# A two-layer macaron block: attention sums kept unturned, reciprocals taken in one small tile, four single banks for the maxima and three for the scores

## The chip, the cores and the metric

The kernel runs on one core of one Trainium2 chip. The metric is the device time of one execution in microseconds (us). Five engines work side by side, each through its own queue in order: TensorE (PE, with its weight loads shown apart as PEld), VectorE (DVE), ScalarE (ACT), GpSimd (POOL) and SyncE (SP), which issues the transfers. They meet at semaphores only. Matmuls write to PSUM, here eight banks of 128 partitions by 512 float32 columns; DVE and ACT read the banks.

## What is computed

The input `x` is 2 x 2048 tokens of 256 features. The reference is a feed-forward, a causal attention and the same feed-forward again, each added to `x`:

```python
x = x + 0.5 * ffn(layernorm(x), W_fc, W_proj)       # relu squared, 1024 hidden, then 5 spiking steps
x = x + attn(layernorm(x), Wq, Wk, Wv, bv, Wo, bo)  # 16 heads of 16, rotary q and k, causal softmax
x = x + 0.5 * ffn(layernorm(x), W_fc, W_proj)
```

The attention is `softmax(q k' / 4, causal) v` for each head, and its output goes through `Wo`. All is float32; products that must be exact are made of three matmuls of high and low parts.

## The kernel before

The program has three stages. The **first feed-forward** takes the tokens in 8 chunks of 512, with projections to q, k and v behind it. The **attention** takes 8 groups (`GROUPS`): 2 sequences by 4 groups of 4 heads. A group has 4 steps `j` of 512 queries, and step `j` has `4j + 4` blocks `b` of 128 keys, so 40 blocks a group (`BLOCKS`) and 320 in all. The **second feed-forward** takes 8 chunks again, with the output projection of the attention ahead of each (`attn_turn`, `attn_out`). All five engines walk the same list of 320 slots, one for each block, each in its own program order.

In slot `g` PE issues (lines 1107 to 1122): some units, the scores of heads 0 and 1, some units, the scores of heads 2 and 3, some units, the products of block `g - 2`, some units. A **unit** (line 1035) is one matmul of queries with keys for one head that only serves to find the largest score of each query; it fills one of `MB = 3` banks of `m_ps`, and DVE takes the maximum out of it (line 971 without mask, line 974 on the diagonal). There are 160 units in a group, placed by `place_units` in the 20 slots before and the 20 after the group's first, mostly 4 or 5 in a slot. The unit `i` may start once DVE has read unit `i - MB`. After the last unit of a step DVE negates the maxima and a **shift** item turns them on PE (line 1052), and SP puts them into the queries as extra rows.

The **scores** (line 1067) of two heads `par = 0, 1` go to the two banks of `s_ps[hp]`, one for each head; the matmuls of `par` 0 and 1 use the upper and the lower half of the array's rows. ACT takes the exponential of both banks in one instruction of up to 1024 columns (line 950). Pair `hp` of block `g` may be written once pair `hp` of block `g - 1` has been read:

```python
wait(pe, exp_done, 2 * block_no(n, j, b) + hp - 1)
```

The last four blocks of a step lie on the diagonal and are 512, 384, 256 and 128 columns wide; POOL sets the masked part to zero. The **products** (line 1082) are the four heads' probabilities times the values, with a column of ones beside the values, so that row 16 of each head's 32 rows in `o_ps` holds the sum of probabilities. At the end of a step ACT copies `o_ps` to `osum` (line 938). A **sums** item then turns `osum` on PE into a bank of `m_ps` (4 transposes, line 1064), DVE takes the reciprocals and multiplies (lines 1005 and 1008), and SP stores token-major `att`. These items stand in the same ring of banks as the units: in slots 7, 15 and 27 of a group and in slot 3 of the next.

In the second feed-forward `load_attn` (line 141) reads the token-major result, PE turns it (8 transposes, line 605), ACT rounds it to `mT_hi` (line 248), DVE makes `mT_lo` (line 362) and `attn_out` projects. Within a chunk's eight steps `f` DVE has its normalisation in `f == 4`, `mT_lo` in `f == 6` and `xT_lo`, for which PE's next chunk waits, in `f == 7` (lines 442 to 489). The first two chunks are prepared within the last group's slots by the `lead` functions.

## Time and profile before

| | |
|---|---|
| median of 3 runs | 1481.79 us (1480.66 to 1482.88) |
| the profiled execution | 1480.84 us |
| its span, first to last instruction | 1479.1 us |
| busy in the span | PE 91%, DVE 77%, ACT 58%, POOL 15% |
| mean granted TensorE clock | 0.949 of 2.4 GHz |
| chain that ended last | PE 74%, DVE 19%, ACT 4% |
| first feed-forward alone | 0 to 309 us |
| its end beside the first units | 309 to 405 us, PEclk 0.67 |
| 300 slots with units | 405 to 1200 us |
| last 20 slots, without units | 1200 to 1252 us |
| second feed-forward | 1252 to 1479 us |

The profiled execution's time lies 1.7 us over its span, and 0.95 us under the median. In the profile a line such as L1049 is the line of the kernel. A busy PE is not a PE at its peak: a matmul's time there includes its weight load and its way through the array, and two matmuls on different halves of the rows overlap.

### The profile page before, as it was taken

What the parts mean: (1) busy time and instruction counts of PE and PEld (TensorE: products, weight loads), DVE (VectorE), ACT (ScalarE), POOL (GpSimd) and SP (SyncE); (2) the same over time, 40 slices, a digit from 0 to 9 for tenths busy, and PEclk for the clock granted to TensorE, in tenths of its full rate; (3) what the DMA queues carried; (4) which work ended last, traced back from release to release, by engine and by line L of the source; (5) the groups of instructions that cost most, each with busy time, mean ns of one, the idle gap of its engine ahead of it and who ended that gap; (6) DMA issues with size and microseconds to landing.
All of it is one profiled execution on the core that took longest, in us unless ns stands there. A gap on an engine that the chain in (4) does not pass through costs nothing.

```text
span 1479.1 us, 22638 instructions
## 1 busy us (share of the span) xinstructions
PE 1345.1 (91%) x8416; PEld 809.8 (55%) x8416; DVE 1134.0 (77%) x2686; ACT 861.4 (58%) x1157; POOL 223.7 (15%) x205
## 2 busy tenths in 40 slices
PE   4988888967799999999999999999999998999996
PEld 3877777854444343444444444443443433999996
DVE  6566776796788888898898898888888851576675
ACT  4654455511166666676666666666666668665664
POOL 4002222241210110110110110110210110101100
PEclk9999999976699999999999999999999999999998
DMA  3123443772272160250340420610701011232312
GB/s 110 48 81 119 136 135 122 149 209 93 72 109 29 27 92 6 39 75 6 56 59 6 75 40 5 91 24 5 106 9 44 9 33 47 76 100 87 99 44 72
DMA packets 98598, 101.41 MB, mean 69 GB/s; under 512 B 39260, under 2 KB 78940, under 8 KB 96860
## 3 DMA queue, kind: packets, MB, share of 16 engines
q1 hardware_dynamic: 98488, 99.97, 29.7%
q8 instruction: 66, 1.08, 0.3%
q14 instruction: 44, 0.36, 0.1%
HBM read 60.16 MB, written 37.75 MB: 66 GB/s over the span
## 4 chain that ended last, share of the span: by engine, by line
PE 74%; DVE 19%; ACT 4%; issue 3%; DMA 0%; POOL 0%; SPq 0%; DVEq 0%; ACTq 0%
PE m_ps L1049 20%; PE o_ps L1094 18%; DVE maxes L971 9%; PE yps_c L563 6%; PE ups_c L545 6%; PE s_ps L1078 5%; PE ups_a L545 5%; PE yps_a L563 4%; PE gps_a L594 3%; DVE masked L974 3%; PE gps_a L579 2%; DVE turned_a L403 2%; PE gps_c L579 2%; ACT probs L950 1%; PE tps_a L572 1%
## 5 line engine op out<-in xcount | busy, mean ns | idle before, releaser
L950 ACT ACTIVATE probs<-s_ps 128x1024 f32<-128x1024 f32 (+3 forms) x640 | 542.0, 896 | 282.6 <-PE s_ps L1078 281.2
L971 DVE TENSOR_REDUCE maxes<-m_ps 128x1 f32<-128x512 f32 x768 | 490.2, 684 | 72.6 <-PE m_ps L1049 70.7
L1049 PE MATMUL m_ps<-kT,qT 64*128 64x512 f32 (+3 forms) x1280 | 455.6, 459 | 56.4 <-DVE maxes L971 37.9
L1049 PEld LDWEIGHTS m_ps<-kT,qT 64*128 64x128 f32 x1280 | 204.2, 192 | 412.1 <-DVE maxes L971 277.6
L1078 PE MATMUL s_ps<-qT,kT 64*128 64x512 f32 (+3 forms) x1280 | 317.0, 404 | 6.8 <-ACT probs L950 6.6
L1094 PE MATMUL o_ps<-probs,v_w 128*32 128x512 f32 (+3 forms) x2560 | 311.1, 559 | 0.1
L974 DVE CUSTOM_DVE_ANT_0 masked<-m_ps,mask 128x384 f32<-128x384 f32 (+3 forms) x512 | 233.6, 485 | 52.7 <-PE m_ps L1049 50.8
L919 POOL TENSOR_SCALAR_AFFINE_SELECT probs<-probs 128x512 f32<-128x512 f32 x128 | 81.3, 635 | 742.0 <-ACT probs L950 742.0
L1078 PEld LDWEIGHTS s_ps<-qT,kT 64*128 64x128 f32 x1280 | 170.0, 192 | 34.0 <-ACT probs L950 28.7
L452 DVE TENSOR_TENSOR h_lo_c<-hsq_c,h_hi_c 128x512 fp32r<-128x512 f32 x64 | 45.0, 703 | 71.1 <-ACT hsq_c L301 35.6
L294 ACT ACTIVATE relu_a<-ups_a 128x512 f32<-128x512 f32 x64 | 38.2, 596 | 99.5 <-PE ups_a L545 98.9
L452 DVE TENSOR_TENSOR h_lo_a<-hsq_a,h_hi_a 128x512 fp32r<-128x512 f32 x64 | 47.3, 739 | 58.5 <-ACT hsq_a L301 36.4
L1094 PEld LDWEIGHTS o_ps<-probs,v_w 128*32 128x32 f32 x2560 | 51.2, 109 | 73.6 <-issue 61.4
L294 ACT ACTIVATE relu_c<-ups_c 128x512 f32<-128x512 f32 x64 | 38.1, 596 | 73.5 <-PE ups_c L545 72.6
L501 POOL TENSOR_TENSOR rot_a<-turned_a 128x512 f32<-128x512 f32 x32 | 42.9, 1362 | 219.9 <-DVE turned_a L403 219.9
L563 PE MATMUL yps_a<-down_hi,h_hi_a 128*128 128x256 f32 x256 | 73.0, 285 | 2.2 <-ACT y_a L288 2.2
L563 PE MATMUL yps_c<-down_hi,h_hi_c 128*128 128x256 f32 x256 | 73.0, 285 | 0.0
L563 PE MATMUL yps_a<-down_lo,h_hi_a 128*128 128x256 f32 x256 | 72.5, 283 | 0.0
L563 PE MATMUL yps_a<-down_hi,h_lo_a 128*128 128x256 f32 x256 | 72.5, 283 | 0.0
L563 PE MATMUL yps_c<-down_hi,h_lo_c 128*128 128x256 f32 x256 | 72.4, 283 | 0.0
L563 PE MATMUL yps_c<-down_lo,h_hi_c 128*128 128x256 f32 x256 | 72.3, 283 | 0.0
L545 PE MATMUL ups_a<-xT_hi_a,up_hi 128*128 128x512 f32 x128 | 54.3, 424 | 2.5 <-DVE xT_lo_a L362 2.5
(128 smaller groups left out, 1923.3 us busy)
## 6 DMA issues: line engine op xcount, KB each, us to landing
qT<-qkT_parts SPq DMA_DIRECT2D x96, 128.0 KB
kT<-qkT_parts SPq DMA_DIRECT2D x48, 256.0 KB
qkT_parts<-qk_hi_a SPq DMA_DIRECT2D x32, 256.0 KB, 4.9
qkT_parts<-qk_lo_a SPq DMA_DIRECT2D x32, 256.0 KB, 4.6
table_a<-in_rot SPq DMA_DIRECT2D x8, 768.0 KB, 7.4
xin_a<-in_x SPq DMA_DIRECT2D x8, 512.0 KB, 3.9
xres_a<-in_x SPq DMA_DIRECT2D x8, 512.0 KB, 4.8
x<-xsum_a SPq DMA_DIRECT2D x8, 512.0 KB, 3.2
```

Of the source, the lines that this page charges most:

```text
L294: act.activation(relu[:, f % 2, :], ups[:, f % 2, :], ACT.Relu).then_inc(s["relu_done"], 1)
L452: dve.tensor_tensor(h_lo[:, f % HB, :], hsq[:, f % 2, :], h_hi[:, f % HB, :].bitcast(F32), ALU.subtract).then_inc(s["lo_done"], 1)
L545: last = pe.matmul(ups[:, f % 2, :], wt[:, c, f * P:(f + 1) * P], x[:, c, :], start=(i == 0), stop=(i == 3 * EC - 1))
L563: last = pe.matmul(yps[:, t, :], h[:, f % HB, t * P:(t + 1) * P], wt[:, f, :], start=(f == 0 and i == 0 and t % 2 == 0), stop=(f == FC - 1 ...
L579: last = pe.matmul(out, x[:, c, t * P:(t + 1) * P], wt[:, c, c0:c1], start=(i == 0), stop=(i == 3 * EC - 1))
L919: pool.affine_select(out=tile, in_=tile, compare_op=ALU.is_ge, fill=0.0, base=0, pattern=[[0, G], [1, P]], channel_multiplier=-1).then_inc ...
L950: act.activation(probs[:, b % PBUF, 2 * hp:2 * hp + 2, off:CH], s_ps[hp][:, :, off:CH], ACT.Exp, scale=D ** -0.5).then_inc(exp_done, 1)
L971: dve.tensor_reduce(out, m_ps[:, i % MB, 0:width], AX.X, ALU.max).then_inc(max_read, 1)
L974: dve.tensor_tensor_reduce(masked[:, i % MB, 0:width], m_ps[:, i % MB, 0:width], mask[:, CH - width:CH], 1.0, NEG, ALU.add, ALU.max, out). ...
L1049: pe.matmul(m_ps[:, i % MB, 0:width], qT[n % 2][r0:r0 + HR, j, hp, t * P:(t + 1) * P], kT[n % 2][r0:r0 + HR, hp, k * CH:k * CH + width], s ...
L1078: mm = pe.matmul(s_ps[hp][:, par, off:CH], kT[n % 2][r0:r0 + HR, hp, b * P:(b + 1) * P], qT[n % 2][r0:r0 + HR, j, hp, off:CH], start=True, ...
L1094: mm = pe.matmul(o_ps[VW * h:VW * (h + 1), off:CH], v_w[n % 2][:, b, h, :], probs[:, b % PBUF, h, off:CH], start=(b == 0), stop=(b == T * ...
```

## The change

The sums are no longer turned. `osum` gets two buffers and is stored as it stands to `sumsT` in DRAM (128 rows a group, transposed). The sums items, `turn_sums` and `normalise` go, and with them the reads of `m_ps` by DVE for them. In the second feed-forward SP loads the sums' rows back into `sums`, already features by tokens, and a copy of the reciprocals of the denominators, spread over 16 rows each, into `denom`. The reciprocals are made once for each chunk on a 128 x 64 tile: SP loads the denominators (`load_denom`), DVE takes the reciprocal (`attn_recip`), SP stores them (`store_recip`). DVE multiplies (`attn_norm`), ACT rounds and DVE makes the low part, both now from SBUF. `attn_turn` goes.

The four banks of scores become three single ones, `s_ps[:, i % 3]`, one for each head in turn. Each head's score matmul signals by itself and waits by itself, and ACT takes one exponential for each head, up to 512 columns. The bank that is freed goes to `m_ps`, which has four.

```diff
-MB = 3
+MB = 4
+SB = 3
...
         def load_attn(c):
...
+            for k in range(EC):
+                sp.dma_start(sums[:, k, :], heads[k, :, 0:D, :]).then_inc(s["a_in"], 16)
+                sp.dma_start(denom[:, k, :], recips[k].unsqueeze(1).broadcast_to([H // EC, D, CH])).then_inc(s["a_in"], 16)
...
+        def attn_recip(c):
+
+            wait(dve, f"denom_in{c % 2}", 16 * (c // 2 + 1))
+            dve.reciprocal(recip[:, c % 2, :], recip[:, c % 2, :]).then_inc(s["a_recip"], 1)
...
+        def attn_norm(c):
+
+            wait(dve, "a_in", 16 * 2 * EC * (c + 1))
+            dve.tensor_tensor(sums[:, :, :], sums[:, :, :], denom[:, :, :], ALU.mult).then_inc(s["a_norm"], 1)
...
                 if f == 4:
                     norm_scale(it + 1)
                     norm("pre", it + 1, it + 1, x2, xn, 0)
+                    if has(it, -2):
+                        attn_norm(it + 2)
+                if f == 5 and has(it, -3):
+                    attn_recip(it + 3)
...
-            if not first and f == 5 and has(it, -2):
-                attn_turn(it + 2)
...
             wait(act, pv_done, g - PBUF + 1)
             for hp in range(2):
-                act.wait_ge(s_done, 2 * g + hp + 1)
-                act.activation(probs[:, b % PBUF, 2 * hp:2 * hp + 2, off:CH], s_ps[hp][:, :, off:CH], ACT.Exp,
-                               scale=D ** -0.5).then_inc(exp_done, 1)
+                for par in range(2):
+                    i = G * g + 2 * hp + par
+                    act.wait_ge(s_done, i + 1)
+                    act.activation(probs[:, b % PBUF, 2 * hp + par, off:CH], s_ps[:, i % SB, off:CH], ACT.Exp,
+                                   scale=D ** -0.5).then_inc(exp_done, 1)
...
-        def turn_sums(e):
-            i = ITEM[e]
-            free_bank(e)
-            pe.wait_ge(o_read, step_no(e[1], e[2]) + 1)
-            for t in range(T):
-                mm = pe.transpose(m_ps[:, bank_of(e), t * P:(t + 1) * P], osum[:, t * P:(t + 1) * P], ident[:, :])
-            mm.then_inc(max_done, 1)
...
-            wait(pe, exp_done, 2 * block_no(n, j, b) + hp - 1)
             for par in range(2):
+                i = G * block_no(n, j, b) + 2 * hp + par
+                wait(pe, exp_done, i - SB + 1)
                 r0 = HR * par
-                mm = pe.matmul(s_ps[hp][:, par, off:CH], kT[n % 2][r0:r0 + HR, hp, b * P:(b + 1) * P],
-                               qT[n % 2][r0:r0 + HR, j, hp, off:CH], start=True, stop=True)
-            mm.then_inc(s_done, 1)
+                pe.matmul(s_ps[:, i % SB, off:CH], kT[n % 2][r0:r0 + HR, hp, b * P:(b + 1) * P],
+                          qT[n % 2][r0:r0 + HR, j, hp, off:CH], start=True, stop=True).then_inc(s_done, 1)
```

The lead of the second feed-forward moves with it: the first two chunks' loads, reciprocals and multiplications stand in slots 2 to 29 of the last group, and the two turns there go.

## Rows read from the trace of the kernel before

**Rows 1.** Windows by stage: length, PE, PEld, DVE, ACT, POOL busy, PEclk, DMA share, GB/s

```profile
405.00:1200.00 795.00, 757.23 (x4921) 323.33 (x4920) 690.52 (x1840) 522.66 (x632) 94.62 (x129) 0.96 0.28 43
1200.00:1252.00 52.00, 46.09 (x311) 17.95 (x312) 10.70 (x27) 39.37 (x48) 9.73 (x10) 0.90 0.18 54
1252.00:1479.00 227.00, 215.55 (x1428) 195.39 (x1426) 147.06 (x260) 133.16 (x222) 17.03 (x6) 0.98 0.25 78
```

**Rows 2.** Waits from 405 to 1200: us in total, times, longest

```profile
DVE maxes L971 <- PE m_ps L1049: 49.5, 142, 0.7
DVE masked L974 <- PE m_ps L1049: 47.9, 97, 1.7
```

**Rows 3.** Timeline of PE's weight loads in one full slot: start us, us, what

```profile
909.94 0.19 PEld L1049 LDWEIGHTS m_ps<-kT,qT 64*128 64x128 f32 x2 [0.84 <-DVE maxes L974]
910.05 0.19 PEld L1078 LDWEIGHTS s_ps<-qT,kT 64*128 64x128 f32 x2
...
911.22 0.18 PEld L1049 LDWEIGHTS m_ps<-kT,qT 64*128 64x128 f32 x1 [0.52 <-DVE maxes L971]
911.65 0.16 PEld L1094 LDWEIGHTS o_ps<-probs,v_w 128*32 128x32 f32 x8 [0.24 <-issue]
912.64 0.19 PEld L1049 LDWEIGHTS m_ps<-kT,qT 64*128 64x128 f32 x2 [0.84 <-DVE maxes L974]
```

**Rows 4.** Timeline of DVE and of ACT in the same slot

```profile
910.48 1.29 DVE L971 TENSOR_REDUCE maxes<-m_ps 128x1 f32<-128x512 f32 x2 [0.20 <-PE m_ps L1049]
...
910.78 1.94 ACT L950 ACTIVATE probs<-s_ps 128x1024 f32<-128x1024 f32 x2 [0.76 <-PE s_ps L1078]
```

**Rows 5.** Groups by shape of line 950: count, busy us, mean ns of one

```profile
L950 ACT ACTIVATE probs<-s_ps 128x512 f32<-128x512 f32 x64 | 35.0, 602 | 14.5 <-PE s_ps L1078 14.5
...
L950 ACT ACTIVATE probs<-s_ps 128x256 f32<-128x256 f32 x64 | 21.2, 381 | 24.1 <-PE s_ps L1078 24.1
```

**Rows 6.** Timeline, last group: exponentials end, two scores that wait, the products behind

```profile
1211.80 3.77 ACT L950 ACTIVATE probs<-s_ps 128x1024 f32<-128x1024 f32 x4 [3.96 <-PE s_ps L1078]
...
1213.79 0.19 PEld L1078 LDWEIGHTS s_ps<-qT,kT 64*128 64x128 f32 x2 [0.73 <-ACT probs L950]
1214.21 0.16 PEld L1094 LDWEIGHTS o_ps<-probs,v_w 128*32 128x32 f32 x8 [0.24 <-issue]
```

**Rows 7.** Timeline, diagonal slot of 256 columns; products of 384 columns and what follows

```profile
932.69 0.29 PEld L1078 LDWEIGHTS s_ps<-qT,kT 64*128 64x128 f32 x2
...
933.36 0.16 PEld L1094 LDWEIGHTS o_ps<-probs,v_w 128*32 128x32 f32 x8
...
934.90 0.16 PEld L1094 LDWEIGHTS o_ps<-probs,v_w 128*32 128x32 f32 x8
935.68 0.19 PEld L1049 LDWEIGHTS m_ps<-kT,qT 64*128 64x128 f32 x2 [0.62 <-DVE maxes L974]
```

**Rows 8.** Timeline of ACT, same diagonal slot

```profile
933.41 1.08 ACT L950 ACTIVATE probs<-s_ps 128x512 f32<-128x512 f32 x2 [1.00 <-PE s_ps L1078]
```

**Rows 9.** First products of two groups in a row, 40 slots apart

```profile
941.00 0.16 PEld L1094 LDWEIGHTS o_ps<-probs,v_w 128*32 128x32 f32 x8 [0.24 <-ACT osum L938]
...
1047.12 0.16 PEld L1094 LDWEIGHTS o_ps<-probs,v_w 128*32 128x32 f32 x8 [0.24 <-ACT osum L938]
```

**Rows 10.** Timeline, the four transposes of a sums item on PE

```profile
943.80 0.42 PEld L1064 LDWEIGHTS m_ps<-ident,osum 128*128 128x128 f32 x4 [0.24 <-issue]
```

**Rows 11.** Waits from 309 to 405

```profile
PE m_ps L1049 <- DVE maxes L971: 21.7, 17, 5.6
```

**Rows 12.** Timeline of DVE, a chunk of the second feed-forward, steps 4 to 7

```profile
1320.70 0.69 DVE L452 TENSOR_TENSOR h_lo_c<-hsq_c,h_hi_c 128x512 fp32r<-128x512 f32 x1 [1.58 <-ACT hsq_c L301]
...
1327.21 0.69 DVE L452 TENSOR_TENSOR h_lo_c<-hsq_c,h_hi_c 128x512 fp32r<-128x512 f32 x1 [0.65 <-ACT hsq_c L301]
...
1330.59 1.22 DVE L362 TENSOR_TENSOR xT_lo_c<-tps_c,xT_hi_c 128x1024 fp32r<-128x1024 f32 x1 [0.42 <-ACT xT_hi_c L248]
```

**Rows 13.** Window at the lower clock, columns as in Rows 1

```profile
1228.00:1232.00 4.00, 4.00 (x20) 0.70 (x12) 1.23 (x1) 3.36 (x5) 0.00 (x0) 0.50 0.37 128
```

More of the change, by code:

```diff
@@ L101, in feed_forward @@
     else:
-        ain, xb, x2, bias = (own[n] for n in ("ain", "xb", "x2", "bias"))
+        sums, recip, denom, xb, x2, bias = (own[n] for n in ("sums", "recip", "denom", "xb", "x2", "bias"))
         split = [("o", own["stage_o"][:, :], proj_hi, proj_lo)]
@@ L222, in body @@
                     store_x2(it + 1)
+                if has(it, -3):
+                    load_denom(it + 3)
+            elif f == FC - 1 and has(it, -3):
+                store_recip(it + 3)
         def end():
@@ L245, in high, with attn_high @@
                 wait(act, "proj_done", 3 * c)
-            if which == "a":
-                wait(act, "o_done", c)
             act.activation(hi[:, :, :], bank[:, :, :], ACT.Copy).then_inc(s[which + "_hi"], 1)
+        def attn_high(c):
+            wait(act, "a_norm", c + 1)
+            wait(act, "o_done", c)
+            act.activation(mT_hi[:, :, :], sums[:, :, :], ACT.Copy).then_inc(s["a_hi"], 1)
         def v_evac(c):
@@ L722, in ring_order @@
             order += [(g, ("unit", n, u)) for u in unit_slots.get(g - BLOCKS * n, [])]
-        order += [(g, ("sums", n, j)) for n in range(GROUPS) for j in range(NJ) if block_no(n, j + 1, SUM) == g
-                  or j == NJ - 1 and block_no(n + 1, 0, SUM) == g]
-    order.append((LAST, ("sums", GROUPS - 1, NJ - 1)))
     for n in range(GROUPS):
@@ L767, in attention @@
     qT, kT, v_in, v_w = ([own[f"{n}{p}"] for p in range(2)] for n in ("qT", "kT", "v_in", "v_w"))
-    probs, ident, bias, mask, masked, maxes, negmax, negparts, shiftT, osum, denom, att = (own[n] for n in (
-        "probs", "ident", "bias_b", "mask", "masked", "maxes", "negmax", "negparts", "shiftT", "osum", "denom", "att"))
+    probs, ident, bias, mask, masked, maxes, negmax, negparts, shiftT, osum = (own[n] for n in (
+        "probs", "ident", "bias_b", "mask", "masked", "maxes", "negmax", "negparts", "shiftT", "osum"))
     s_ps, m_ps, o_ps = banks
@@ L822, in moves @@
                     shift(n, j)
-                elif what == "sums":
+            for n, j in steps():
+                if g == min(block_no(n, j, T * j + T) + STORE, LAST):
                     store(n, j)
@@ L933, in read_sum @@
         def read_sum(n, j):
+            t = step_no(n, j)
             act.wait_ge(pv_done, block_no(n, j, T * j + T))
-            if (n, j) != (0, 0):
-                act.wait_ge(max_done, ITEM["sums", (NJ * n + j - 1) // NJ, (j - 1) % NJ] + 1)
-            act.activation(osum[:, :], o_ps[:, :], ACT.Copy).then_inc(o_read, 1)
+            wait(act, osum_out[j % 2], 16 * (t // 2))
+            act.activation(osum[:, j % 2, :], o_ps[:, :], ACT.Copy).then_inc(o_read, 1)
         def slot(g):
@@ L1126, in end @@
                 products(*SLOTS[g])
-        def last_sums():
-            ring(ITEMS[LAST])
-        return slot, end, last_sums
+        return slot, end
     return sync, scalar, vector, gpsimd, tensor
@@ L1184, in build @@
     b["probs"] = memory.take("probs", [P, PBUF, G, CH])
-    b["osum"] = memory.take("osum", [P, CH])
+    b["osum"] = memory.take("osum", [P, 2, CH])
     assert memory.at <= rest
@@ L1204, in build @@
     memory = Memory(nc, probs)
-    for n in ("xres", "xsum"):
-        c[n] = memory.take(n + "_c", [P, T, E])
+    for n, shape, dt in (("xres", [P, T, E], F32), ("xsum", [P, T, E], F32), ("count", [P, T * E], BF16)):
+        c[n] = memory.take(n + "_c", shape, dt)
     with ExitStack() as ctx:
```

172 lines of the change are left out of this document (84 added, 88 removed).

## The prediction

> **What bounds the kernel now.** I read the windows by stage first, then the waits of the longest stage, then the timelines of one slot, engine by engine. 795 of the 1479 us lie in the 300 slots of attention that have units, 52 in the last 20 slots, 227 in the second feed-forward [rows 1]. In the long stage PE is busy 757 us, DVE 691, ACT 523. So PE and DVE are both near full, and what counts is how they hand over to each other. DVE waited 49.5 + 47.9 = 97 us for units, in 239 waits of 0.4 us [rows 2].
>
> One full slot shows the loop. PE loads two units at 909.94 and the first scores at 910.05, then waits at its last unit until 911.22, because with three banks it must let DVE finish the first unit of this slot; the products start at 911.65 and take 0.99 us, and the next slot's units start at 912.64: 2.70 us [rows 3]. DVE starts on the first unit at 910.48 after 0.20 us of idleness [rows 4]. The loop is: unit to DVE 0.54, DVE's read and the way back 0.74, last unit to products 0.43, products 0.99. ACT is no part of it: it starts the pair's exponential at 910.78, waited 0.76 us for it, and has done by 912.72 [rows 4]. A whole group of 40 slots takes 1047.12 - 941.00 = 106.1 us, 2.65 a slot [rows 9]; the seven such pairs lie between 106.0 and 107.1.
>
> **Four banks for the units and no sums items** take this loop away. The last unit now waits for a unit of the slot before, which DVE has read long ago. A sums item costs PE 0.42 us for its transposes [rows 10], and one unit more waits behind it. If nothing came in its place, the 97 us would shrink and some 0.6 us for each of 30 sums items would go.
>
> **Three single score banks** put a new wait in its place, and this is the step on which I decide. The four scores of slot g have the numbers 4g to 4g + 3, and score i waits until exponential i - 3 is done. So the fourth score waits for the first exponential of its own slot. Before, the second pair waited only for the slot before. The price, from rows:
> - First score's load to ACT's start: 910.05 to 910.78, 0.73 us [rows 3, 4].
> - One exponential of 512 columns: 0.60 [rows 5].
> - End of an exponential to the load of a score that waits for it: the second of four back to back ends at 1211.80 + 0.92 + 1.02 = 1213.74 (four take 3.77, so each but the last adds 0.92), and the load is at 1213.79: 0.05 [rows 6].
> - Load of a late score to the products: 1213.79 to 1214.21, 0.42 [rows 6]. The unit between them shares that time if it uses the other half of the rows.
> - Products 0.99, and products' end to the next first score 0.11 [rows 3].
>
> Together 0.73 + 0.60 + 0.05 + 0.42 + 0.99 + 0.11 = 2.90 us for a full slot, whatever DVE does; it was 2.70. The loop goes PE to ACT to PE once a slot, and PE stands about 1.0 us at the fourth score with the remaining units, the products and all of the next slot queued behind it. DVE has then more than it can use, and ACT, with four exponentials at 0.48 (two take 1.08, one 0.60 [rows 5, 8]) and one tail, needs 2.04 of the 2.90.
>
> On the diagonal the loss is larger, as these slots were short. With 256 columns: first score to ACT 932.69 to 933.41, 0.72 [rows 7, 8]; exponential 0.38 [rows 5]; then 0.05 + 0.42. So the products come 1.57 us after the first score, where they came 0.67 after it [rows 7]. For 384 columns I take 0.62 + 0.49 and for 128 0.60 + 0.27, estimates from the same rows' slope of 0.86 ns a column, with 0.25 instead of 0.42 behind the narrowest.
>
> The group's sum: products 28 x 0.99 + 4 x (0.78 + 0.57 + 0.36) = 34.6 (0.78 for 384 columns, 934.90 to 935.68 [rows 7], 0.21 less for each 128 columns fewer); first score to fourth score 28 x 1.38 + 4 x (1.16 + 1.15 + 0.92) = 51.6; fourth score to products 36 x 0.42 + 4 x 0.25 = 16.1; turn of the slot 40 x 0.11 = 4.4. That is 106.7. On top come units beyond four in a slot, the shift items, and a unit on the same half of the rows as the fourth score: 0 to 5 us, I take 3.7, since ten slots or so have each of these at 0.1 to 0.2. **110.4 for 106.1**, so +4.3 a group. Crowded slots, in which PE waited most for DVE, gain; quiet and diagonal ones lose more. 300 slots are 7.5 groups: **+32 us** (bounds: 0.2 us less or more in the hand-overs of each slot, -28 to +92 against the time before).
>
> **The last 20 slots** have no units. Today ACT binds them with pairs of exponentials at 0.92 each, 1.84 a slot [rows 6]. A full slot now needs 0.60 + 0.60 + 0.05 + 0.42 + 0.99 = 2.66. Fourteen full slots and six diagonal ones come to 50, and the chunk's projection, one turn and ACT's table loads stand in between for some 8: 58 for 52 [rows 1], **+6** (3 to 15).
>
> **The stretch before 405.** PE waited 21.7 us there for DVE to free a bank, in 17 waits [rows 11]. One more bank lets it run one read of 0.6 us further each time, part of which DVE's long work takes back: **-4** (-12 to 0).
>
> **The second feed-forward** is PE's alone. Six turns of 8 transposes (two of the 8 chunks' were in the lead) go, at about 0.42 for four [rows 10]: -5. But DVE gets a multiplication of 128 x 1024 in step 4, for which I take the 1.14 that `xT_lo` adds [rows 12], and a reciprocal of 64 columns in step 5, no row of this size, between 0.2 and 1 us, I take 0.5. From step 4's start at 1320.70 to the end of `xT_lo` at 1331.81 are 11.1 us, and the free time in it is 0.65 + 0.42 [rows 12]; so `xT_lo` comes 0.6 us later, and PE waits for it at the next chunk. The turns' gain is then not to be had: six times 0.5, less 0.6 for the last sums item, **+2** (-6 to +8). The added loads, four for one and two small ones for each chunk, are issued a chunk ahead and hide behind it; SP's queue waits in `load_attn` for a store of reciprocals, with `load_x` and the stores behind, none needed within a step. If that cover failed, a load's few us would stand in front of each of six chunks. Uncovered nowhere: the single `osum` copies and their stores.
>
> **Sum.** 1480.84 + 32 + 6 - 4 + 2 = 1516.8; the median lay 0.95 above the profiled execution: **1518 us**.
>
> A page speaks to the scores' signals: in the Trainium skill, "TensorE: Matmul & The Clock Gate", section "The cost: per-tile semaphore tail", increments of tiles that run side by side serialise at 26 ns each. Each pair now signals twice. An estimate by that page would be 0.03 us in each of 320 slots, 8 us more; no row here parts the two.
>
> **Rival one: the fourth score's wait hides** (0.18). It would if the first exponential's release came 0.2 us earlier than I have it, at 1.18 instead of 1.38 us after the first score: then a full slot is below today's 2.70, and the gain of the banks shows. For it: today's completion is that of a pair, and a single head's may come sooner. Against: both heads stream side by side, and the terms are all measured. With half of DVE's 97 us and half of the sums items' 20 or so gone, the time is about 1420, at the very least 1365.
>
> **Rival two: the clock** (0.13). PE's work in a slot stays, the slot grows, so PE idles more. In the last group the granted clock is 0.50, which is 1.2 GHz, from 1228 to 1232 [rows 13], behind a stretch in which PE had waited for ACT; over the last 20 slots it is 0.90 [rows 1]. At that level products take about 0.9 us longer, and with the scores a slot some 1.3. If 30 to 60 slots fall so, +40 to +75: 1555 to 1590. The Trainium skill says the same, "TensorE: Matmul & The Clock Gate", section "A second HAM failure mode: psum-queue depth-cycling": small idle gaps between groups of matmuls let the clock swing between its levels. By that rule the last 20 slots are the first to fall.
>
> **Rival three: the two loops balance** (0.12): the crowded slots gain what the quiet ones lose. 1479 to 1494; of this 0.05 is within 0.2%, about what a measurement of this kernel can tell from no change.
>
> **How the numbers follow.** Forecast, 1495 to 1545: 0.55. Rival one 0.18, rival two 0.13, rival three 0.12, something slower yet 0.02. Faster 0.18, same 0.05, slower 0.77. The range runs from 1479 to 1572: it holds the forecast, rival three and most of rival two.
>
> **What would show it.** Right: in a full slot of units two loads of scores close together, a third, and the fourth about 1.4 us after the first, with "ACT probs" as its releaser; full slots of 2.9 us and hardly any that differ by their number of units; DVE's waits for `m_ps` not gone but longer, ACT's exponentials in runs of one to three; diagonal slots of 2.3 to 2.8. Wrong: the fourth score's load within 0.5 us of the first, DVE back to back. The second feed-forward is right if PE waits for `xT_lo` by 1 us or more each chunk.

## The result, and the profile after

The changed kernel took **1576.04 us** (1571.72 to 1584.23, 4 runs), the kernel before 1481.32 (1480.66 to 1482.88, 4 runs) beside it: ratio 1.0644, 95% interval 1.0599 to 1.069. Slower, as forecast, but by 95 us where 36 were forecast, and 4 us above the range. The profiled execution took 1577.86 with a span of 1576.1; the four runs order themselves by their mean granted clock: 1571.72 at 0.938, 1574.22 at 0.937, 1577.86 at 0.934, 1584.23 at 0.928.

The windows of the changed kernel, with the columns of [rows 1]:

```profile
405.00:1200.00 795.00, 686.03 (x4424) 280.19 (x4423) 623.80 (x1661) 514.84 (x1127) 86.25 (x116) 0.96 0.28 46
```

In the same 795 us PE gets through 4424 matmuls, before it was 4921. The waits of that window (us in total, times, longest):

```profile
PEld s_ps L1098 <- ACT probs L992: 201.6, 273, 1.2
...
DVE masked L1016 <- PE m_ps L1076: 83.4, 119, 2.5
DVE maxes L1013 <- PE m_ps L1076: 82.0, 139, 1.9
```

Now 273 slots have a score that waits for ACT, 0.74 us each. DVE's waits for units, 97 us in [rows 2], are 165: four m banks did not let DVE run on, since PE, which fills them, stands at the score. One full slot shows it. PE's weight loads:

```profile
1262.01 0.19 PEld L1098 LDWEIGHTS s_ps<-qT,kT 64*128 64x128 f32 x2
...
1262.25 0.18 PEld L1098 LDWEIGHTS s_ps<-qT,kT 64*128 64x128 f32 x1
1263.38 0.18 PEld L1098 LDWEIGHTS s_ps<-qT,kT 64*128 64x128 f32 x1 [0.95 <-ACT probs L992]
...
1263.80 0.16 PEld L1113 LDWEIGHTS o_ps<-probs,v_w 128*32 128x32 f32 x8 [0.24 <-ACT probs L992]
...
1264.91 0.19 PEld L1098 LDWEIGHTS s_ps<-qT,kT 64*128 64x128 f32 x2
```

and ACT's exponentials of the same slot:

```profile
1262.73 2.06 ACT L992 ACTIVATE probs<-s_ps 128x512 f32<-128x512 f32 x4 [0.84 <-PE s_ps L1098]
```

Two scores, a third, and the fourth 1.37 us after the first with ACT's `probs` as releaser; from first score to first score 1264.91 - 1262.01 = **2.90 us**, the forecast's number, against 2.70 in [rows 3]. ACT starts 0.72 after the load. So the mechanism stands, and the question is where the other 60 us are.

These two are slots with nothing on top. Taken over all full slots of this stage that lie at the full clock (512 columns in the scores and in the products; 142 of them after, 140 before), the median goes from 2.71 to 3.06 us and the mean only from 2.97 to 3.09, since the slots before spread from 2.20 to 4.48 and those after from 2.78 to 3.84.

I split both spans at three places: the first products, those 297 slots later, and those of the slot before the last two. Before, the three stand at 409.80, 1197.14 and 1249.79, after at 406.47, 1266.70 and 1335.15. The two middle stretches, before and then after, as windows with the columns of [rows 1]:

```profile
409.80:1197.14 787.34, 752.13 (x4899) 320.85 (x4898) 684.79 (x1825) 517.06 (x625) 93.35 (x127) 0.97 0.28 43
1197.14:1249.79 52.65, 45.48 (x295) 17.30 (x295) 13.24 (x35) 39.48 (x48) 8.71 (x9) 0.90 0.18 54
...
406.47:1266.70 860.23, 742.67 (x4779) 302.67 (x4778) 672.45 (x1769) 555.26 (x1219) 93.23 (x127) 0.95 0.27 44
1266.70:1335.15 68.45, 57.10 (x276) 20.56 (x274) 18.46 (x34) 43.22 (x89) 9.31 (x9) 0.78 0.20 59
```

| stretch | before | forecast | after | after, PE kept at work (experiment e6_fill) |
|---|---|---|---|---|
| to the first products | 409.8 | -4 | -3.3 | -3.8 |
| slots with units | 787.3 | +32 | +72.9 | +46.2 |
| last 20 slots | 52.65 | +6 | +15.8 | +10.9 |
| from there to the end of the span | 229.3 | +2 | +11.6 | +10.0 |
| sum | 1479.1 | +36 | +97.0 | +63.2 |

Between the same products of one group and the next lie 118.7, 114.8, 113.5, 120.4, 112.4, 114.5 and 113.9 us, where before all were within 106.0 to 107.1 [rows 9]. A loop gives every group the same; something in the changed kernel comes and goes. The granted clock goes with it: its mean is 0.90 in the group of 120.4 us and 0.92 in that of 118.7, and 1.00 in that of 112.4. The kernel before is not free of this either: each of its groups has a mean of 0.97 or 0.95. Two windows of 4 us behind the narrow diagonal slots at the start of a group, columns as in [rows 1]:

```profile
520.00:524.00 4.00, 3.32 (x30) 1.68 (x30) 3.76 (x8) 3.42 (x9) 2.10 (x3) 1.00 0.76 169
...
528.00:532.00 4.00, 3.67 (x16) 1.31 (x15) 1.50 (x6) 1.33 (x5) 0.63 (x1) 0.50 0.99 116
```

The granted clock (the column before the last two) falls from 1.00 to 0.50, which is 1.2 GHz, behind slots in which PE waited 0.6 to 0.8 us for ACT each; by 532 it is back. In between full products take 1.86 us:

```profile
525.21 0.20 PEld L1113 LDWEIGHTS o_ps<-probs,v_w 128*32 128x32 f32 x8 [0.24 <-issue]
527.07 0.28 PEld L1076 LDWEIGHTS m_ps<-kT,qT 64*128 64x128 f32 x1 [1.66 <-issue]
```

against 0.99 in [rows 3].

### The profile page after: what moved, and what is told of

Read it like the earlier page. It is cut to its first block and busy times, and to the rows that moved or that the text cites. A ratio compares the mean times of both kernels' runs of the same rounds, so it can differ in the third digit from the quotient of the medians.

```text
span 1576.1 us, 22827 instructions
## 1 busy us (share of the span) xinstructions
PE 1344.9 (85%) x8224; PEld 792.7 (50%) x8224; DVE 1135.1 (72%) x2638; ACT 902.6 (57%) x1797; POOL 222.5 (14%) x205
## 5 line engine op out<-in xcount | busy, mean ns | idle before, releaser
L992 ACT ACTIVATE probs<-s_ps 128x512 f32<-128x512 f32 (+3 forms) x1280 | 585.6, 542 | 330.0 <-PE s_ps L1098 326.7
L1098 PE MATMUL s_ps<-qT,kT 64*128 64x512 f32 (+3 forms) x1280 | 407.7, 417 | 120.8 <-ACT probs L992 120.4
L1076 PE MATMUL m_ps<-kT,qT 64*128 64x512 f32 (+3 forms) x1280 | 405.8, 441 | 23.4 <-DVE maxes L1013 15.2
L1098 PEld LDWEIGHTS s_ps<-qT,kT 64*128 64x128 f32 x1280 | 206.0, 195 | 266.9 <-ACT probs L992 249.6
L1076 PEld LDWEIGHTS m_ps<-kT,qT 64*128 64x128 f32 x1280 | 186.3, 193 | 271.8 <-DVE maxes L1013 152.0
L1113 PE MATMUL o_ps<-probs,v_w 128*32 128x512 f32 (+3 forms) x2560 | 319.8, 574 | 0.0
L1113 PEld LDWEIGHTS o_ps<-probs,v_w 128*32 128x32 f32 x2560 | 51.6, 110 | 84.3 <-ACT probs L992 42.9
L622 PE MATMUL yps_c<-down_hi,h_hi_c 128*128 128x256 f32 x256 | 72.9, 285 | 0.0
L605 PE MATMUL ups_c<-xT_hi_c,up_hi 128*128 128x512 f32 x128 | 54.2, 423 | 11.2 <-DVE xT_lo_c L398 11.2
```

What stands on the lines that cost most here:

```text
L605: last = pe.matmul(ups[:, f % 2, :], wt[:, c, f * P:(f + 1) * P], x[:, c, :], start=(i == 0), stop=(i == 3 * EC - 1))
L622: last = pe.matmul(yps[:, t, :], h[:, f % HB, t * P:(t + 1) * P], wt[:, f, :], start=(f == 0 and i == 0 and t % 2 == 0), stop=(f == FC - 1 ...
L992: act.activation(probs[:, b % PBUF, 2 * hp + par, off:CH], s_ps[:, i % SB, off:CH], ACT.Exp, scale=D ** -0.5).then_inc(exp_done, 1)
L1076: pe.matmul(m_ps[:, i % MB, 0:width], qT[n % 2][r0:r0 + HR, j, hp, t * P:(t + 1) * P], kT[n % 2][r0:r0 + HR, hp, k * CH:k * CH + width], s ...
L1098: pe.matmul(s_ps[:, i % SB, off:CH], kT[n % 2][r0:r0 + HR, hp, b * P:(b + 1) * P], qT[n % 2][r0:r0 + HR, j, hp, off:CH], start=True, stop= ...
L1113: mm = pe.matmul(o_ps[VW * h:VW * (h + 1), off:CH], v_w[n % 2][:, b, h, :], probs[:, b % PBUF, h, off:CH], start=(b == 0), stop=(b == T * ...
```

## The experiments

The theories: the loss is the loop through the first exponential of the slot (A), with the clock's fall on top of it; it is the splitting of signals and exponentials as such (C); or it comes from the sums' new path. Times are medians; the kernel before beside each group of runs took 1483.43, 1482.76 and 1482.62.

### Unturned sums alone

The changed kernel with three m banks, two double score banks and exponentials of 1024 columns, as before.

```
-MB = 4
-SB = 3
+MB = 3
+SB = 4
...
-                for par in range(2):
-                    i = G * g + 2 * hp + par
-                    act.wait_ge(s_done, i + 1)
-                    act.activation(probs[:, b % PBUF, 2 * hp + par, off:CH], s_ps[:, i % SB, off:CH], ACT.Exp,
+                act.wait_ge(s_done, 2 * g + hp + 1)
+                act.activation(probs[:, b % PBUF, 2 * hp:2 * hp + 2, off:CH], s_ps[:, 2 * hp:2 * hp + 2, off:CH], ACT.Exp,
...
```

> Only the unturned sums and their reciprocals of the change; the scores stay in two double banks with exponentials of 1024 columns, the units in three banks. Theory A (the wait of the fourth score on the first exponential of its own slot is most of the cost): full slots with four units are back at 2.70 us, the sums items' four slots a group fall by 0.6 to 1.1 us each, so the 300 slots take 770 to 780 us (795 before, 860 after the change); the second feed-forward keeps its 12 us loss. Together 1465 to 1480 us. Theory B (the sums' new way through DRAM and SBUF is what costs): 1520 us or more.

Measured: **1465.65 us** (1463.85 to 1466.87), ratio 0.9878 (0.9863 to 0.9892). Unturned sums are a gain of 17.8 us; the whole loss, 110 us against this run, is the banks' part. Its groups also show what the clock costs. Two in a row, the first with a stretch at 0.50 and the second without:

```profile
721.84:825.27 103.43, 98.34 (x645) 41.52 (x644) 89.80 (x241) 69.66 (x85) 12.52 (x17) 0.97 0.30 48
825.27:926.47 101.20, 95.99 (x645) 40.47 (x644) 89.70 (x241) 69.39 (x85) 12.52 (x17) 1.00 0.30 49
```

The same 40 slots take 2.2 us more with 6.8 us of them at 0.50, so each us at the lower clock costs about 0.33. The kernel before has 6.8 such us in each group but the first, so its group would be about 103.9 at the full clock and not 106.1, by this estimate.

Where the banks' loss falls can be read from the same comparison, slot by slot at the full clock: the 21 full slots of a group take 60.8 us here and 64.9 in the changed kernel, the 19 on the diagonal or with narrow products 40.5 and 47.2. The larger part is in the narrow slots, which have the same round trip through ACT and less work to share it.

### Four single score banks, three m banks

The changed kernel with `MB = 3` and `SB = 4`: each head signals, waits and has its exponential by itself, but the fourth score waits only for the slot before.

> As the first, but with four single score banks, a signal and a wait for each head and exponentials of 512 columns; the fourth score then waits for an exponential of the slot before. Theory A: no slot of its own waits, so within 10 us of the first kernel, 1465 to 1490, and the loads of the four scores lie within 0.5 us. Theory C (twice as many exponentials and signals cost by themselves): the first kernel's time plus 0.1 us or more a slot, 1505 us or more.

Measured: **1468.66 us** (1467.07 to 1472.24), ratio 0.9902 (0.9887 to 0.9918), 3.0 us above the run before it. By the trace its full slots have 2.70 us again. Theory C is out: splitting 640 exponentials into 1280 costs 3 us. By the Trainium skill ("TensorE: Matmul & The Clock Gate", "The cost: per-tile semaphore tail") I had estimated 8 us for the doubled signals alone. Between the two runs signals, waits and exponentials together cost 3.0, of which the slots with units have 765.4 - 763.5 = 1.9, so the estimate is not borne out here. It had also counted one increment more in a slot, where the change makes two.

### Three m banks with three single score banks

```
-MB = 4
+MB = 3
```

> The changed kernel with three m banks in place of four (the eighth bank lies idle). Theory: in the changed kernel the fourth score's wait binds nearly every slot, so the fourth m bank earns next to nothing there: within 15 us of the changed kernel's 1576, somewhat more where a unit now waits behind the fourth score. The first products come some 3 us later (the stretch before 405, where the fourth bank gave 3.3). Rival: the fourth bank carries much of the changed kernel's slots (crowded ones of five to eight units above all), and without it the unit loop of 2.70 us adds to the score loop: 1610 or more.

Measured: **1619.58 us** (1614.8 to 1631.25), ratio 1.0938 (1.0889 to 1.0986). My expectation missed, the rival was right: the changed kernel is 43.5 us faster for its fourth m bank. With the two runs before it this is a ladder with one thing changed at each step: before 1483, unturned sums -18, splitting +3, **one score bank fewer +151**, one m bank more -44, changed kernel 1576. These steps hold the clock's price too: from the first products on, the 297 slots with units have 133 us at 0.50 in this run, 78 in the changed kernel and 35 with four single score banks. At 0.35 us each (see the next but one run) some 19 of the 44 and 34 of the 151 are the clock's, by estimate. The median full slots of four units are as in the changed kernel (2.91 and 3.13 us). The difference lies in the crowded ones. One with five units and narrow scores, weight loads in this run:

```profile
1072.35 0.29 PEld L1076 LDWEIGHTS m_ps<-kT,qT 64*128 64x128 f32 x3 [0.84 <-DVE maxes L1016]
1073.26 0.18 PEld L1076 LDWEIGHTS m_ps<-kT,qT 64*128 64x128 f32 x1 [0.61 <-DVE maxes L1016]
1073.27 0.29 PEld L1098 LDWEIGHTS s_ps<-qT,kT 64*128 64x128 f32 x2
...
1074.89 0.16 PEld L1113 LDWEIGHTS o_ps<-probs,v_w 128*32 128x32 f32 x8 [0.19 <-ACT probs L992]
```

and the same slot in the changed kernel:

```profile
1040.33 0.30 PEld L1076 LDWEIGHTS m_ps<-kT,qT 64*128 64x128 f32 x4 [0.84 <-DVE maxes L1016]
1040.56 0.19 PEld L1098 LDWEIGHTS s_ps<-qT,kT 64*128 64x128 f32 x2
...
1042.08 0.16 PEld L1113 LDWEIGHTS o_ps<-probs,v_w 128*32 128x32 f32 x8 [0.19 <-ACT probs L992]
```

With three banks the first scores stand behind a unit that waits for DVE, 0.92 us after the slot's first load and not 0.23; the wait for ACT comes after it, and the two add up: 2.54 us to the products, and 1.75 with four banks.

### Two score banks

```
-SB = 3
+SB = 2
```

> Dose test of the ring's loop. The changed kernel with two score banks in place of three: score i waits until exponential i - 2 is done. By my theory (a slot is the loop first score, exponentials, late score, products, next first score) the third score then waits for the slot's first exponential and the fourth for its second. In the changed kernel a full slot was 0.73 + 0.60 + 0.05 + 0.42 + 0.99 + 0.11 = 2.90 us; one more exponential back to back, 0.48, stands in it now: 3.38 at least, so +0.5 us or more in each of 320 slots: 1576 + 160 = 1736, expected between 1700 and 1780, and the fourth score's load about 1.9 us after the first. By the rival (the loss comes from something that does not hang on the ring's length: the split of the exponentials, the sums' new path, the clock alone) it stays between 1560 and 1620.

Measured: **1776.07 us** (1774.97 to 1796.31), ratio 1.2011 (1.1946 to 1.2075). A full slot:

```profile
1445.20 0.19 PEld L1098 LDWEIGHTS s_ps<-qT,kT 64*128 64x128 f32 x2
...
1446.57 0.18 PEld L1098 LDWEIGHTS s_ps<-qT,kT 64*128 64x128 f32 x1 [0.95 <-ACT probs L992]
1447.06 0.18 PEld L1098 LDWEIGHTS s_ps<-qT,kT 64*128 64x128 f32 x1 [0.30 <-ACT probs L992]
...
1448.60 0.19 PEld L1098 LDWEIGHTS s_ps<-qT,kT 64*128 64x128 f32 x2
```

The third score waits for the first exponential, the fourth for the second, 0.49 later, and the slot is 3.40: the loop is longer by one exponential and nothing else. The total goes to the upper end of what was expected because the mean clock sinks to 0.879 as well: the slots with units are 186 us longer than in the changed kernel, with 213 us more at 0.50, which is about 75 of the 186 by the price of the next run.

### PE kept at work in its wait

The third score's matmul is issued three times, with one signal behind the last.

```
-                pe.matmul(s_ps[:, i % SB, off:CH], kT[n % 2][r0:r0 + HR, hp, b * P:(b + 1) * P],
-                          qT[n % 2][r0:r0 + HR, j, hp, off:CH], start=True, stop=True).then_inc(s_done, 1)
+                for _ in range(3 if (hp, par) == (1, 0) else 1):
+                    mm = pe.matmul(s_ps[:, i % SB, off:CH], kT[n % 2][r0:r0 + HR, hp, b * P:(b + 1) * P],
+                                   qT[n % 2][r0:r0 + HR, j, hp, off:CH], start=True, stop=True)
+                mm.then_inc(s_done, 1)
```

> Tests the clock's part. The changed kernel with the third score's matmul issued three times into its bank with the same result, so that PE works for some 0.8 us of the 1.0 us in which it stands at the fourth score; the loop is left as it is. Clock theory: of the 72.9 us that the 300 slots of attention grew by, some 20 to 25 are slots at 1.2 GHz; with PE kept at work the granted clock rises from 0.934 to 0.95 or more, the full slots stay at 2.90 to 3.15, the groups that took 114 to 120 us come to about 112, and the total is 1535 to 1560. Rival (the clock has no part, the extra is made by waits between the engines): 1570 or more, the filler only in the way. If the filler delays the unit behind it, the slots at full clock become longer by up to 0.2 us and part of the gain is lost.

Measured: **1544.03 us** (1542.95 to 1548.45), ratio 1.0419 (1.0402 to 1.0436): 640 matmuls more, and 32 us less than the changed kernel. The stretch with units and the last 20 slots, as in [rows 1]:

```profile
405.96:1239.48 833.52, 814.60 (x5373) 389.47 (x5372) 671.04 (x1769) 556.13 (x1220) 93.55 (x127) 1.00 0.27 46
1239.48:1303.03 63.55, 58.40 (x317) 26.34 (x315) 16.61 (x34) 43.29 (x89) 9.64 (x9) 0.89 0.22 63
```

The mean granted clock of the slots with units is 1.00, 0.95 without the filler; all but the first 2 us of them are at 1.00. The seven groups take 113.0, 112.4, 112.1, 112.4, 112.3, 112.1 and 112.4 us: the coming and going is gone, and what is left is the loop. A full slot still has 2.90 or 3.13, and the one group that had the full clock without the filler took 112.4 too, so the filler itself costs nothing there. It gives back 26.7 us in the slots with units (72.9 - 46.2), 4.9 in the last 20, and 32 in all. With 77.8 us at 0.50 gone down to 2.2, that is 0.35 us for each. (These lengths are from the clock's record, of which the windows show two rounded digits.)

The 26.7 us are what the clock costs the changed kernel, not what the change added. The kernel before has 51.6 us at 0.50 in the same slots, about 17 us by the 0.33 of the first run, and no run has it at the full clock. So of the +72.9 some 10 are the clock's and some 63 the loop's, as an estimate. And in the last 20 slots the filler did its work only in part: 13.7 us at 0.50 are left there, of 30.7.

### The fourth score behind the products

```
-            scores(n, j, b, 1)
+            scores(n, j, b, 1, (0,))
...
                 products(*SLOTS[g - 2])
+            scores(n, j, b, 1, (1,))
```

> The changed kernel with the fourth score issued behind the products instead of ahead of them, nothing else. By then the first exponential is done, so Theory A says that the 1.0 us at the fourth score goes: full slots fall from 2.90 to 2.4 to 2.5 us, where DVE's four reads are the bound, a group from 112 to 98 to 103, and the kernel to 1450 to 1490 us. If something else made the slots long (the split exponentials, the lower clock by itself), the time stays over 1550.

Measured: **1496.46 us** (1486.35 to 1500.2), ratio 1.0083 (1.0057 to 1.0108). 80 us come back, though less than I expected. A full slot:

```profile
1181.55 0.18 PEld L1098 LDWEIGHTS s_ps<-qT,kT 64*128 64x128 f32 x1 [0.84 <-ACT probs L992]
...
1181.66 0.41 PEld L1098 LDWEIGHTS s_ps<-qT,kT 64*128 64x128 f32 x2
...
1182.73 0.18 PEld L1098 LDWEIGHTS s_ps<-qT,kT 64*128 64x128 f32 x1 [0.48 <-ACT probs L992]
...
1183.39 0.16 PEld L1113 LDWEIGHTS o_ps<-probs,v_w 128*32 128x32 f32 x8 [0.37 <-ACT probs L992]
1184.39 0.18 PEld L1098 LDWEIGHTS s_ps<-qT,kT 64*128 64x128 f32 x1 [0.84 <-ACT probs L992]
```

The fourth score no longer waits, but now the next slot's third score does, for the exponential of that fourth: 1.18 us, then 0.66 to the products and 1.00 for them, 2.84 in all. The wait has moved to the other place where three scores stand in a row without the products between them.

### The products between the two pairs of scores

```
             ring(items[q[1]:q[2]])
-            scores(n, j, b, 1)
-            ring(items[q[2]:q[3]])
             if g >= 2:
                 products(*SLOTS[g - 2])
+            ring(items[q[2]:q[3]])
+            scores(n, j, b, 1)
```

> The changed kernel with another order of PE's work in a slot: the first pair of scores, a unit, the products of the slot before, the other units, the second pair of scores. The banks, the exponentials and all the work stay. By my theory (the cost is where the fourth score's wait stands, not the three banks as such) the wait of 1.4 us for the first exponential now runs beside 0.99 us of products and the units, so the loop through ACT drops out, and DVE or ACT bound the slot at 2.4 to 2.6 us: 300 slots save 60 to 130 us against the changed kernel: 1440 to 1500, so at or below the time before of 1482. Rival (three single banks cost their time wherever the wait stands, as each score still needs an exponential of its own slot): 1540 to 1580. What could spoil it: the second pair of scores then ends the slot and the next slot's first pair waits for the second and third exponentials; that would show as waits of the first pair on ACT, and a time between 1500 and 1540.

Measured: **1524.79 us** (1517.05 to 1525.78), ratio 1.0272 (1.0246 to 1.0299). The spoiling that the expectation named is what came:

```profile
1209.40 0.29 PEld L1098 LDWEIGHTS s_ps<-qT,kT 64*128 64x128 f32 x2
...
1209.96 0.18 PEld L1098 LDWEIGHTS s_ps<-qT,kT 64*128 64x128 f32 x1
1210.80 0.18 PEld L1098 LDWEIGHTS s_ps<-qT,kT 64*128 64x128 f32 x1 [0.66 <-ACT probs L992]
...
1211.46 0.16 PEld L1113 LDWEIGHTS o_ps<-probs,v_w 128*32 128x32 f32 x8 [0.36 <-ACT probs L992]
```

The second pair and the next slot's first score come at once, the next one waits for the exponential of the third head: 1210.80 - 1209.40 = 1.40 us, the same price as ever, and the products stand behind it again. Wherever one block of products is put, one score stands three behind another without it.

### The products in two halves

The changed kernel with the earlier normalisation (below); a full block's products cut into 2 x 256 columns, with the fourth score between the halves.

```
+            for c0, c1 in ((0, CH // 2), (CH // 2, CH)) if off == 0 and b > 0 else ((off, CH),):
+                if c0 == CH // 2 and off == 0:
+                    between()
+                for h in range(G):
+                    mm = pe.matmul(o_ps[VW * h:VW * (h + 1), c0:c1], v_w[n % 2][:, b, h, :],
+                                   probs[:, b % PBUF, h, c0:c1], start=(b == 0), stop=(b == T * j + T - 1))
```

> The changed kernel's banks and exponentials, the normalisation early, and the products of a full block cut into two halves of 256 columns. Order in a slot: first pair of scores, unit, third score, first half of the products, fourth score and its unit, second half, unit. By the run with the products in the middle, the loop through ACT is whole wherever three scores stand behind one another without the products between them; that run had 3.07 us for a full slot, as the changed order only moved the wait to the next slot's second score. With a half between any score and the third behind it, each wait of 1.38 us has 0.57 us of products, and mostly a unit and other scores, beside it. From rows: first score to fourth 1.38, half of the products 0.57, turn 0.11, a unit or two between: 2.1 to 2.3, so that DVE's 0.6 for each of four units binds: 2.4 to 2.55 a full slot, where it was 2.90. The cut costs 0.15 of products. Expected 1430 to 1490. Rival: each wait for ACT costs its time in full however the work is cut, as the engine's queue in order stands behind it: 1520 or more.

Measured: **1501.34 us** (1499.79 to 1510.67), ratio 1.0143 (1.0103 to 1.0183), between the two theories. Full slots take 2.48 us where the fourth score's unit uses the other half of the rows, and 2.92 where it uses the same. One of the latter:

```profile
916.09 0.16 PEld L1117 LDWEIGHTS o_ps<-probs,v_w 128*32 128x32 f32 x8 [0.36 <-issue]
916.65 0.18 PEld L1098 LDWEIGHTS s_ps<-qT,kT 64*128 64x128 f32 x1 [0.41 <-ACT probs L992]
...
917.32 0.16 PEld L1117 LDWEIGHTS o_ps<-probs,v_w 128*32 128x32 f32 x8 [0.37 <-issue]
917.88 0.19 PEld L1076 LDWEIGHTS m_ps<-kT,qT 64*128 64x128 f32 x2 [0.41 <-issue]
```

The fourth score comes right behind the first half, as the unit does behind the second half with nothing to wait for (0.41 of idleness both times). The loop through ACT is broken. What binds is PE: 0.56 for each half, and each half is followed by a turn, 0.67 here from the late score to the second half.

### Unturned sums, normalisation early; and the same with split products

DVE's multiplication in step 3 of a chunk and not 4, the reciprocals in step 2 and not 5. First in the changed kernel:

```
-                    if has(it, -2):
-                        attn_norm(it + 2)
-                if f == 5 and has(it, -3):
+                if f == 3 and has(it, -2):
+                    attn_norm(it + 2)
+                if f == 2 and has(it, -3):
```

> The changed kernel with DVE's multiplication in step 3 and its reciprocal in step 2 of a chunk instead of steps 4 and 5. Theory D (ACT, which waits in step 5 for the multiplication, is late for the squares behind it, and so PE gets its next chunk late): ACT's wait for the multiplication and PE's 11 us of waits for xT_lo go, the turns' 5 us show, and the time falls by 10 to 17 us, to 1559 to 1566. If DVE's added work by itself is the cost, wherever it stands, it stays within 3 us of 1576.

Measured: **1566.89 us** (1558.42 to 1569.84), ratio 1.0546 (1.0511 to 1.0581), 9 us less. The rows that it bears on, in the second feed-forward of the changed kernel:

```profile
ACT mT_hi_c L284 <- DVE sums_c L409: 15.4, 6, 2.6
PEld ups_c L605 <- DVE xT_lo_c L398: 12.7, 7, 2.2
```

and in this run, where ACT's row for `sums_c` is gone:

```profile
PEld ups_c L605 <- DVE xT_lo_c L398: 2.6, 7, 0.6
```

The stretch behind attention falls from 241.0 to 225.4 us. That is 15.6 and not 9; the slots with units, which the edit leaves alone, took 6 us more in the profiled execution, with 98 us at 0.50 for 78.

Then the same edit with unturned sums alone:

> Unturned sums alone (three m banks, two double score banks and exponentials of 1024 columns as before) gave 1465.65; there the stretch from the end of attention still lasted 238 us, 10 longer than before, which I put down to the normalisation in the fourth step of a chunk, for which ACT's rounding of the sums waits in step five. This kernel is that one with the normalisation one step earlier and the reciprocals three steps earlier. In the changed kernel this edit gave 9 us. Theory: the same here, 1453 to 1459. Rival (PE has then something else to wait for in that stage, or the sooner normalisation holds up DVE's earlier work): 1462 to 1467.

Measured: **1451.22 us** (1449.8 to 1452.67), ratio **0.9791** (0.9774 to 0.9807), the fastest of all. It gave 14.4 us, more than expected, and close to the 15.6: from the products of the slot before the last two to the end of the span are 224.3 us, 239.7 without it, 229.3 in the kernel before. Here at last the turns' 5 us are had.

Last, this kernel with the split of the products, the last unit between the halves, against the unit loop of 2.70:

> The fastest so far (unturned sums alone with the early normalisation, three m banks, double score banks: 1451) with the products of full blocks cut into two halves of 256 columns and the last unit put between them. Theory: the loop of the kernel before, unit to DVE 0.54, DVE's read and the way back 0.74, last unit to products 0.43, products 0.99, is 2.70; with 0.57 of products in it in place of 0.99 it is 2.28, and DVE's four units at 0.6 bind: 2.4 to 2.55 in some 120 full slots, where they took 2.70. Gain 15 to 30 us: 1420 to 1437. Rival: PE has no free time for a second set of weights and the 0.15 us more of products, and the slots stay at 2.70 or grow: 1450 to 1475.

Measured: **1476.07 us** (1473.28 to 1477.93), ratio 0.9956 (0.9939 to 0.9974): 25 us more than without it, the rival, and beyond its 1475. Two halves with a unit between them:

```profile
886.37 0.16 PEld L1115 LDWEIGHTS o_ps<-probs,v_w 128*32 128x32 f32 x8 [0.25 <-issue]
886.94 0.18 PEld L1074 LDWEIGHTS m_ps<-kT,qT 64*128 64x128 f32 x1 [0.41 <-DVE maxes L1014]
887.31 0.16 PEld L1115 LDWEIGHTS o_ps<-probs,v_w 128*32 128x32 f32 x8 [0.19 <-issue]
887.88 0.18 PEld L1074 LDWEIGHTS m_ps<-kT,qT 64*128 64x128 f32 x1 [0.41 <-issue]
```

From the first half to what follows the second are 1.51 us, where whole products take 0.99. The cut costs 0.15, as reckoned, and a second turn from a unit to products 0.37 more; I had reckoned with the loop through DVE and not with what PE itself then has to do. Full slots gain nothing (2.69 for 2.70), quiet ones lose (1.89 to 2.23 in one with three units).

## Why the prediction was wrong, step by step

**The loop: right to the hundredth in the plain slot.** First score to fourth 1.38, measured 1.37; fourth to products 0.42, measured 0.42; a full slot 2.90, measured 2.90. Two banks and four banks moved it as the ring's rule says: 3.40, and back to 2.70. "DVE has then more than it can use" held too, and so did "on the diagonal the loss is larger". The sign "hardly any that differ" did not: full slots run from 2.78 to 3.84, with a median of 3.06.

**The clock: the step that failed.** I had it as a rival with 0.13, at 1555 to 1590, as if the forecast and it excluded each other, and put it at nothing in the sum. But the loop itself makes the idleness that lets the clock fall, so the likeliest case was both, and the clock's price belonged into the sum. All terms of the 110.4 us a group hold for the full clock, and the 106.1 that I subtracted from it was a group with 6.8 us at 0.50 in it. The changed kernel spends 78 us at 0.50 in the slots with units, which cost it 26.7, and 30.7 in the last 20 slots, some 11 by the estimate below: 37 in all, of which e6_fill gives back 32. My 40 to 75 was a little too much for the clock: the price of a slot was near (1.46 us for a full one, 4.13 against 2.67 in the last 20, where I had 1.3), but only some 25 slots fell and not 30 to 60. The total of the rival came out near for another reason, the terms below that the forecast had too small. (1518 plus 40 to 75 is also 1558 to 1593 and not 1555 to 1590.) I had named the last 20 slots as the first to fall. By the share of their time they are hit hardest (0.50 from 1270 to 1280, 0.58 from 1290 to 1310); of the whole they have about a third, and most of the rest is behind the narrow, quiet slots at a group's start, as in the windows above. The Trainium skill's rule of small gaps between groups of matmuls ("TensorE: Matmul & The Clock Gate", "A second HAM failure mode: psum-queue depth-cycling") agrees with the traces here: filling the gaps alone brought the clock from 0.95 to 1.00 in the slots with units. The kernel before had 0.97 there.

**The loop's sum over a group: 110.4 forecast, 112.3 at full clock.** Against the 106.1 as measured that is +6.2 where +4.3 was forecast, and against a group before at the full clock, 103.9 by the estimate above, some +8.4. The terms of the plain slots hold; the extras over 106.7 were 5.6 and not 3.7. Most of them, 4.2 in the group from 873.96 to 986.38, lie between the fourth score and the products. About half of the 5.6 is the unit on the same half of the rows as the fourth score. I gave it 0.1 to 0.2, and it is 0.25 in each of about ten slots: there the fourth score is no later, but the products are, 0.67 behind it where they were 0.42.

```profile
1062.57 0.19 PEld L1098 LDWEIGHTS s_ps<-qT,kT 64*128 64x128 f32 x2
...
1063.94 0.18 PEld L1098 LDWEIGHTS s_ps<-qT,kT 64*128 64x128 f32 x1 [0.72 <-ACT probs L992]
...
1064.61 0.16 PEld L1113 LDWEIGHTS o_ps<-probs,v_w 128*32 128x32 f32 x8 [0.37 <-ACT probs L992]
```

Over 7.5 groups this is the 14 us between +32 and +46.2.

**The last 20 slots: +6 forecast, +15.8, or +10.9 with the filler.** This too is the clock, and not the chunk's own work. At the full clock a full slot takes 2.66 to 2.67, the forecast's 2.66, and at 0.50 it takes 4.13, so each us at 0.50 costs 0.35. Without the 30.7 us at 0.50 the 68.45 are 57.6, without the 13.7 the 63.55 are 58.7, and the forecast was 58; these are estimates. The chunk's work has one odd row: DVE's low part of the sums, 1.22 us elsewhere, took 3.12 beside POOL's addition of the bias.

```profile
1274.00 3.12 DVE L414 TENSOR_TENSOR mT_lo_c<-sums_c,mT_hi_c 128x1024 fp32r<-128x1024 f32 x1 [1.82 <-ACT mT_hi_c L284]
...
1273.70 2.35 POOL L573 TENSOR_TENSOR xb_c<-xin_c,bias_c 128x1024 f32<-128x1024 f32 x1
```

It costs the stretch nothing that shows. It ends at 1277.12, and PE loads the first weights of the output projection 4.4 us later, straight behind products at the lower clock:

```profile
1281.48 0.29 PEld L638 LDWEIGHTS gps_c<-proj_hi_c,mT_hi_c 128*128 128x128 f32 x1 [1.66 <-issue]
```

With unturned sums alone the same operation takes 3.14 beside POOL, and there the last 20 slots are 4.0 us shorter than before.

**The second feed-forward: +2 forecast, +11.6.** Durations were right (multiplication 1.22 for 1.14, reciprocal 0.55 for 0.5), and so was the sign that I named, PE's wait for `xT_lo`; its size was 12.7 us in 7 waits, 1.8 us a chunk, where it was 1.4 us in all before, and I had 0.6 a chunk. The step that failed is the wait that the change adds on ACT. Its queue runs in order, and `mT_hi` stands in it ahead of `relu`, `hsq` and `xT_hi`:

```profile
1412.18 1.06 ACT L284 ACTIVATE mT_hi_c<-sums_c 128x1024 fp32r<-128x1024 f32 x1 [2.56 <-DVE sums_c L409]
```

I summed DVE's work in the step and forgot that ACT would stand 2.6 us for it, with DVE's next inputs queued behind. The earlier normalisation took the wait away in both kernels, and with it 15.6 and 15.4 us of this stretch. Not all of that is the wait itself: the changed kernel also has 13.7 us at 0.50 in the second feed-forward before the end of its work, and neither the kernel before nor either kernel with the earlier normalisation has any. What they cost is not parted from the wait.

**Before 405: -4 forecast, -3.3.** Right; without the fourth m bank the first products come at 410.96, 4.5 us later. **The cover of the loads:** right, no wait for them shows in the chunks' chain. POOL does wait 104.5 us for loads of `x` in this stage, but nothing then waits for POOL.

**What kept the range too narrow:** with 14 for the loop's extras, 8 for the wait on ACT and the 5 us of the clock that the filler leaves in the last 20 slots, 1518 becomes 1545 (e6_fill: 1544), and with the 32 that the filler gives back 1577. Two of the three misses are of mechanism (the clock, the wait on ACT), one of size (the loop's extras).

## What to carry to other kernels

In a ring with fewer banks than a slot has users, write down for each user the one that many places before it in the engine's order: its whole round trip through the other engine stands in the slot unless enough work lies between the two, and moving the work only moves the place. Where a change adds a wait to PE and the trace of before already shows its granted clock falling behind such waits, the clock's price is a term of the sum, not a case beside it, and the time before holds some of it too. And for each wait that an edit adds, list what stands behind it on that engine's own queue.

## What the runs showed of the hardware that I had not expected

- The same work with 640 matmuls more is 32 us faster (1544.03 for 1576.04), as the granted clock of the slots with units stays at 1.00.
- A us at the lower clock costs this kernel a third of a us: 0.33 and 0.35 in the slots with units, 0.35 in those without.
- From the load of a 64 x 128 unit or score with 512 columns to the load of 128 x 32 products behind it pass 0.37 to 0.67 us, and they are paid again with each cut of the products; that is what cutting them costs, more than the 0.15 of the second set of loads.
- A DVE operation on SBUF took 3.12 us beside POOL's 2.35 us addition, where it takes 1.22 alone. It ended 1.07 us behind the end of POOL's (1277.12 and 1276.05), and 1.08 behind it with unturned sums alone (1183.61 and 1182.53), as if it had stood until POOL was done.
- The way back from ACT to PE is short: the first exponential of the full slot above ends at 1262.73 + 0.60 = 1263.33, and the score that waited for it is loaded at 1263.38.
